# Input, residual and output of a batch in one of three rotating buffers, and the feed-forward additions placed behind the projections, in a two-layer transformer kernel

## The reference

```
x = layernorm(x + linear_attention(x))      # L0: gram matrix of Q and K, x + gamma * V-term
x = layernorm(x + moe(x))                   # 8 experts, gate softmax, threshold 0.1, dense
x = layernorm(x + head_attention(x))        # per token: 16 heads attend to 16 heads (dh 16), /8
x = layernorm(x + routed_ffn(x))            # top 75% of each 2048 tokens: gelu(x @ w_block), others x
```

## Time and profile before

| | us |
|---|---|
| median of 3 runs (1372.45 to 1375.73) | 1373.98 |
| the profiled execution, its own time | 1370.22 |
| its span in the trace | 1368.3 |
| PE busy | 1168.1 (85%) |
| DVE busy | 934.5 (68%) |
| ACT busy | 722.7 (53%) |
| POOL busy | 579.6 (42%) |
| one turn with all three batches | 155.3 to 156.5 |

### The profile page before, as it was taken

The page is one execution under the profiler, slowest core; times in us unless marked ns, Lnnn a source line. Parts: engine busy times, 40 slices in busy tenths (PEclk is TensorE's granted clock), DMA queues, the critical chain, the costliest instruction groups (busy, mean ns, idle before and its releaser), DMA issues.

```text
span 1368.3 us, 31179 instructions
## 1 busy us (share of the span) xinstructions
PE 1168.1 (85%) x12264; PEld 749.3 (55%) x12264; DVE 934.5 (68%) x2116; ACT 722.7 (53%) x1146; POOL 579.6 (42%) x886
## 2 busy tenths in 40 slices
PE   6588898998989899998999899998989988995643
PEld 4444456655665556655665546555656544653532
DVE  3544677577866867677866867677766867657845
ACT  3222475347753575447753575537853575545434
POOL 3135335435435446336344356245354345252242
PEclk8799998899979998899979998799978998698556
DMA  5000091205702193203902084202902066108230
GB/s 185 16 2 15 31 158 15 78 9 114 111 9 71 32 172 31 79 8 99 126 2 78 17 175 43 79 9 82 143 2 63 1 154 63 38 26 151 37 93 31
DMA packets 93145, 90.64 MB, mean 66 GB/s; under 512 B 7110, under 2 KB 81864, under 8 KB 92744
## 3 DMA queue, kind: packets, MB, share of 16 engines
q1 hardware_dynamic: 80648, 75.54, 29.7%
q0 software_dynamic: 2560, 8.39, 1.8%
q10 hardware_dynamic: 9792, 4.72, 1.5%
HBM read 46.68 MB, written 41.94 MB: 65 GB/s over the span
## 4 chain that ended last, share of the span: by engine, by line
PE 38%; DVE 20%; POOL 11%; ACT 10%; DMA 9%; issue 8%; SPq 3%; ACTq 1%; POOLq 0%; DVEq 0%
PE bank L1848 36%; DMA ct<-scratch_qkv 4%; POOL stage L647 4%; SPq L520 3%; DVE keys L1546 2%; DMA bt<-scratch_o 2%; ACT shared L796 2%; DMA scratch_o<-stage 2%; DVE x L1435 2%; DVE stats L1294 2%; POOL rs L597 2%; DVE gelu L1548 2%; DVE ct L1264 1%; ACT x L920 1%; PE bank L1858 1%
## 5 line engine op out<-in xcount | busy, mean ns | idle before, releaser
L1848 PE MATMUL bank<-we,at 128*128 128x512 f16 x1536 | 372.2, 401 | 1.9 <-DVE x L1435 1.9
L1848 PEld LDWEIGHTS bank<-we,at 128*128 128x128 f16 x1536 | 154.0, 102 | 193.5 <-issue 40.0
L612 POOL TENSOR_TENSOR part<-part 128x512 f32<-128x512 f32 x64 | 83.7, 1308 | 273.3 <-ACTq L946 273.3
L796 ACT ACTIVATE part<-bank,wexp 128x256 f32<-128x256 f32 x256 | 104.6, 472 | 162.7 <-PE bank L1848 108.6
L1435 DVE SCALAR_TENSOR_TENSOR x<-bank,wexp,x 128x256 f32<-128x256 f32 x256 | 122.7, 479 | 53.5 <-PE bank L1848 47.0
L1848 PE MATMUL bank<-bt,wqkv 128*128 128x512 f16 x576 | 138.8, 383 | 21.3 <-DVE stage L1264 15.6
L920 ACT ACTIVATE x<-x,nm,rs 128x256 f32<-128x256 f32 x192 | 104.6, 593 | 90.8 <-POOL nm L600 89.6
L1264 DVE TENSOR_TENSOR stage<-bank,stage 128x512 f16<-128x512 f32 x112 | 75.6, 686 | 83.8 <-ACT stage L796 83.6
L593 POOL TENSOR_SCALAR nm<-mv 128x2 f32<-128x2 f32 x128 | 35.3, 276 | 226.6 <-DVE mv L1299 220.9
L1848 PE MATMUL bank<-keys,blockdiag 128*128 128x16 f16 x3072 | 97.1, 193 | 19.7 <-issue 15.6
L1848 PEld LDWEIGHTS bank<-keys,blockdiag 128*128 128x128 f16 x3072 | 95.7, 104 | 24.4 <-issue 22.8
(11 more groups left out here) (189 smaller groups left out, 2247.9 us busy)
## 6 DMA issues: line engine op xcount, KB each, us to landing
scratch_qkv<-stage SPq DMA_DIRECT2D x40, 512.0 KB, 3.3
ct<-scratch_qkv SPq DMA_DIRECT2D x112, 128.0 KB, 7.1
x_in<-in_x_dram SPq DMA_DIRECT2D x32, 256.0 KB, 2.8
keys<-scratch_qkv SPq DMA_DIRECT2D x64, 128.0 KB, 6.1
bt<-scratch_o SPq DMA_DIRECT2D x16, 512.0 KB, 3.7
out_dram<-x POOLq DMA_DIRECT2D x32, 256.0 KB, 2.7
scratch_qkv<-part SPq DMA_DIRECT2D x8, 512.0 KB, 8.3
scratch_o<-stage SPq DMA_DIRECT2D x32, 128.0 KB, 3.6
```

Of the source, the lines that this page charges most:

```text
L612: pool.tensor_tensor(part[:, 0:2, :], part[:, 0:2, :], part[:, 2:4, :], ALU.add)\
L796: return act.activation(dst, src, ACT.Copy, scale=scale)
L1848: ins = pe.matmul(dst, lhs, rhs, start=(n == 0), stop=(n == len(terms) - 1))
```

## The change

The three buffers become `xb[0..2]`. Batch n lives in `xb[n % 3]` from its load to its store: the linear attention writes its result over the input, and everything that followed in `x1` and `x3` happens in place. POOL's four copies in a turn are gone, with the waits of `a_apn` and `b_pr` for them. The input of batch a goes where batch a-3 was, so its load now waits for that batch's stores, pair by pair. In SP's list it stands behind F7, F9 and F11's stores and ahead of the load of the keys.

The diff, cut (each use of `x_in`, `x1`, `x2`, `x3_of(b)` became `x_of(n)`; PE's list is described below):

```diff
-        x_in = sb("x_in", [P, T, D])
+        xb = [sb(f"xb{i}", [P, T, D]) for i in range(3)]
...
@@ SP, load_x and turn @@
+                if a >= 3:
+                    sp.wait_ge(out_stored[p], 16 * (a - 2))
+                    sp.sem_inc(waits_held, 1)
...
                     b_loadq(b)
                     b_f(b, 7)
+                    if more:
+                        load_x(a, 0)
+                        load_x(a, 1)
                     b_f(b, 9)
+                    if more:
+                        load_x(a, 2)
                     b_f(b, 11)
+                    if more:
+                        load_x(a, 3)
                     b_loadk(b)
                     b_loadv(b)
...
@@ POOL @@
-            def b_copy(b, p):
-
-                pool.wait_ge(x2_ready, 4 * b + p + 1)
...
+                    ln(b, 7, 0)
+                if a is not None:
+                    ln(a, 0, 0)
+                    ln(a, 1, 0)
                 if c is not None:
                     ln(c, 4, 1)
...
+                    b_store(c, 0)
                     ln(c, 5, 1)
-                    b_store(c, 0)
...
                     b_store(c, 1)
...
                     ln(c, 6, 1)
...
+                if a is not None:
+                    ln(a, 2, 0)
+                if c is not None:
+                    b_store(c, 2)
                     ln(c, 7, 1)
...
+                if a is not None:
+                    ln(a, 3, 0)
+                if c is not None:
                     b_store(c, 3)
@@ ACT @@
-                if later(a):
-                    act.wait_ge(b_full, b_filled(a - 1, f"TX{p}"))
-                    act.wait_ge(x3_copied, 4 * (a - 1) + p + 1)
```

221 lines of the change are left out of this document (100 added, 121 removed).

## The result

The changed kernel takes **1390.35 us** (median of 4 runs, 1388.79 to 1392.68); before took 1373.22 beside it. The ratio is 1.0134, with a 95% interval from 1.0107 to 1.0160: slower by 17 us, where I had forecast 6.4 (1380, range 1365 to 1395). The profiled execution took 1392.68, with a span of 1390.8.

A forecast was written before the change was run, and what follows sets the result against it. Gate on PE, first turned q on ACT and landed values decide a turn. 9.5 + 0.1 - 3.2 = +6.4 on the profiled 1370.22 gives 1376.6; that execution stood 3.8 below the median, so about 1380, range 1365 to 1395.

The forecast's parts named there:

- F0 to TY3: Rank to gate: F0 leads by 4.8 us, POOL's strict order turns that into a gate 2.8 us late.
- The clock: Rival, chance 0.15: PE idle between F10 and TY3 drops to 1.2 GHz, 2.6 us in each of five turns, 1393.
- The last input load lands at 816.7 or a little later: Past the gate: load waits for store 3, issued 813.9; turned q then starts at 817.6 instead of 814.29.
- The next term: Past the gate: values alone take 11.5 us, landing at 836.6 to 836.7; chain 1.9 us late per turn.
- The buffers themselves cost nothing: Whole kernel: the buffers cost nothing; the removed copies were also priced at 0, at most 2.5 us a turn.
- -3.2 for the load of `bt`: Closing part: two input loads no longer ahead of this load shorten PE's wait, -3.2 us in all, bounds -3.2 and 0.
- Turn 1 has no `c`: 0: Turn 1: no cost, 0 us, since it has no `c`.
- Turn 7, +0.1: Turn 7: without `a_xs`, turned q comes 3 us late, yet the turn loses only 0.1 us.
- the values then land with the keys' bound: Turn 7: the landing of the values is set by the keys, not by the late turned q, +0.1 us.
- step past the gate: From gate to landed values: the chain is 1.9 us late per turn, bounds 0.1 and 3.3, over five turns 9.5.
- The whole lead: Rival, chance 0.07: store 2 doesn't hold POOL, gate 4 us early, a turn gains about 4.5 us, 1344.
- Nothing to measure: Rival, chance 0.16: values land by DMA rate alone, +0.5 us a turn or less, -0.6 in all, 1373.

The follow-up runs named there:

- e1: The changed kernel with POOL's third store moved behind ln(c, 7, 1) and ln(a, 3, 0): 1379.82 us, 1.0060.
- e8: e1 with all four input loads of a full turn together ahead of F9's and F11's stores: 1369.75 us, 0.9982.
- e11: e8 with POOL's store 1 behind the sums for c6 and a2, and ACT's cast of TY3 ahead of the last feed-forward normalisation: 1372.74 us, 0.9995.
- e5: The kernel before with three rotating buffers, no copies and SP's new load places, all other orders as before: 1392.43 us, 1.0153.
- e6: e5 with all four input loads of a full turn together ahead of F9's and F11's stores, behind the query loads: 1379.77 us, 1.0066.
- e12: e6 with the four input loads ahead of the query loads and F7's store: 1366.30 us, 0.9946.
- e9: The changed kernel with VectorE's a_cb_lo(a) ahead of a_ln2(b, 3) again, in turn 1 alone: 1391.00 us, 1.0147.
- e7: The changed kernel with the full turns' four stores issued by SP instead of POOL, and all input loads ahead of F9's store: 1377.34 us, 1.0051.
- e10: The changed kernel with all four input loads of a full turn together ahead of F9's and F11's stores, POOL's order unchanged: 1388.39 us, 1.0117.
- e13: e11 with the gate weights' cast ahead of input casts 1 and 2, and the last cast between the turned query's halves: 1372.87 us, 0.9998.
- e4: The changed kernel with 12 extra matmuls filling PE's wait between F10 and TY3: 1385.85 us, 1.0090.

## Why the prediction was right in its sign and off in its size

**F0 to TY3: right.** F0 at 780.63 (780.7), apn2 at 800.97 (801.0), apn3 at 807.71 (807.75), TY3 at 808.79 (808.75), the gate 2.91 us late in the mean (2.85; in this one turn 3.6, with F11 at the lower clock). POOL's strict order does it: e1, which only moves store 2 behind two sums, takes the gate back to 36.16 and gains 10.5 us.

**The clock: it fell, mostly elsewhere, and the price of the rival isn't seen.** The rival had it fall between F10 and TY3 in each turn and F11 and gate the slower for it. It did so in turn 5 alone, behind the gate in turns 2, 4, 6 and 7, and not in turn 3, with the same wait ahead of TY3 in all six. The transpose of the gate's selection comes 3.3 (turn 3) to 4.6 us late, where the gate is 2.9 late. Up to the turned values that costs the turn nothing that shows. In the turn of the rows PE waits 2.75 us, at 867.08, for the first product made from the turned values (1.83 before), so what a slower PE lost ahead of it lies in a wait. e8 has the fall behind the gate in all six turns, and the turned values at 61.55; e11 doesn't have it there, and they come at 62.94. Behind the turned values it is not so clear. Every kernel here spends 20 us or more of each turn at the lower clock there, before some 24 and the changed kernel 20 to 30, and single turns last from 92.1 to 95.9 us from the turned values on. What part the clock has in that no run separates. The 1393 of this rival is nearest to the measured 1390, and by the number only.

**"The last input load lands at 816.7 or a little later": the term that was mis-sized.** I let it go out when store 3 had landed, and take 2.8 us. It goes out 0.5 us later than that, behind F11's store, takes 4.71 and lands at 819.16. The turned query is 4.5 us late in the mean and not 3.3. The next term, 11.5 us from the issue of the values to their landing, was right (11.57 in the mean to the turned values), so the chain is 2.6 us late per turn instead of 1.9. Over five turns that is 3.5 us.

**"The buffers themselves cost nothing": a statement on causes that failed.** In the sum it did no harm, since the layout had the load in its chain, as a follower of store 3. But e5 shows that the buffers with these load places cost 21 us by themselves, with before's POOL order and an early store 3. The price isn't the buffer but the place on SP's queue: two loads behind F9's and F11's stores 21 us (e5), all behind the query loads 8 (e6), ahead of them -7 (e12). What e12's 7 us are is open. The copies, priced at nothing, may be it: e12's values are issued 0.3 us and turned 1.1 us earlier than before's, and turn 1 is 0.8 shorter. Or the two loads that left the load of `bt`: PE's waits for it are 1.1 us in e12 and 3.5 before. No run here has one without the other.

**"-3.2 for the load of `bt`": not seen at the end.** The wait did shrink. A view like that of rows 11, over a little more of the trace (200 to 1210 us), gives PE's matmuls 3.5 us in five waits before and 0.9 in one after. But the stretch from the turned values to the end of the turn is 93.63 against 93.30: whatever that wait was worth, something else took it. I expected 3.2 less, and 0.3 a turn more came: 4.9 us over five turns.

**"Turn 1 has no `c`: 0": wrong, +2.1.** The new order stands there too. All kernels with it have 153.1 to 154.3, all with the old one 149.9 to 151.1. In this turn F0 starts 0.6 us late and the gate 4.0 (34.64 against 30.63), of which 1.3 is F11, now ahead of it; the turned query is then 3.8 late and the turned values 2.2, as much as the turn. Which of the moves does the rest is open: e9 took back the one whose wait I saw, and a wait came back one step on.

**Turn 7, +0.1: too small.** The turned query comes 4.5 us late there (45.01 against 40.53), and the turned values 1.5 (64.08 against 62.56). That "the values then land with the keys' bound" doesn't hold: they stand behind the turned query here too.

6.4 + 3.5 + 4.9 + 2.1 gives 16.9. That is what turns 1 to 6 differ by in the two traces (16.7), taken apart, and not an account of the medians' 17: the traces themselves are 22.5 apart. For turn 0 nothing is claimed: it lies between 104.1 and 108.3 in these executions, without regard to the edits. That the forecast's range holds is in part luck. Its step past the gate was too small (1.9 us a turn for 2.6), what it took off for `bt` didn't come, and turn 1 wasn't in it. The upper bound covers these only because it let all of ACT's delay go through (3.3 a turn) and left room beyond.

**What the experiments leave of the rivals.** "The whole lead" (1344) came in no run: in e7 and e11 the gate is 0.6 to 0.9 earlier than before, not 4, and it doesn't set the end. "Nothing to measure" is by its number what both repairs together give (e8), not by its reason.

## What to carry to other kernels

A load that gets a new wait gets its place in a queue with it: ask what stands ahead of it on the issuing engine, what is already in the DMA engines when it goes out, and what stands behind its first reader. When one delay is repaired and half of the loss stays, look for a second that lies beside it before doubting the first; the square of e1, e8, e10 has two such edits at 2 (within the noise) and 10.5 us alone and 20.6 together. And measure from fixed points in each turn: here one of them, the start of the turned values, told a turn's mean length within 0.7 us in fourteen kernels, while PE's gate, which I had timed to 0.1 us, did not: e5 has it early and is the longest. And look at a clock in every turn: the one I had picked was the only one of six where it fell ahead of TY3.

## What the runs showed of the hardware

- An input load of 256 KB landed after 2.8 us in the median before: 2.7 in windows in which the DMA share was 0.3 to 0.4, 5.5 where it was 0.95 (at 883.21). Beside key loads it took 4.7 to 5.9 us (the changed kernel, e5), and behind query loads and a store on the same queue 10.2 (e6).
- The DMA engines had a full share both at 112 GB/s, with the query loads under way, and at 368 GB/s, 6 us later (e6).
- The same eight value loads, issued 49.1 to 49.8 us behind the start of the turn, kept POOL waiting from 6.65 to 9.49 us over five turns of one execution (e13).
- The same program with the same wait of 3.08 to 3.09 us met the fall of TensorE's clock at different places: ahead of TY3 in one turn (0.69, then 0.50), behind the gate in four, in one not at all (the changed kernel). With the gap filled, four of six turns still had it (e4).
